# Cross attention on TensorE: the mixing products moved ahead of the next batch's key products in each slot

## The reference, cut to what matters

```python
# b = 32 batches, 100 queries, 722 context rows, 16 heads of 32
qh = (q @ wq + bq).reshape(b, -1, H, HD).transpose(0, 2, 1, 3)
kh = (k @ wk + bk).reshape(b, -1, H, HD).transpose(0, 2, 1, 3)
vh = (v @ wv + bv).reshape(b, -1, H, HD).transpose(0, 2, 1, 3)
scores = softmax(einsum('bhqd,bhkd->bhqk', qh, kh), axis=-1)
attn = einsum('bhqk,bhkd->bhqd', scores, vh)
```

## Time and profile before

| what | us |
|---|---|
| median of 3 runs | 2761.03 |
| lowest, highest | 2760.5, 2762.95 |
| the profiled execution | 2773.05 |
| its span, first to last instruction | 2771.2 |
| TensorE's matmuls busy in it | 2619.4 (95%) |
| VectorE, ScalarE busy | 1819.4 (66%), 1334.0 (48%) |

### The profile page before, as it was taken

The page is one execution under the profiler, slowest core; times in us unless marked ns, Lnnn a source line. Parts: engine busy times, 40 slices in busy tenths (PEclk is TensorE's granted clock), DMA queues, the critical chain, the costliest instruction groups (busy, mean ns, idle before and its releaser), DMA issues. The chain is left out here.

```text
span 2771.2 us, 48090 instructions
## 1 busy us (share of the span) xinstructions
PE 2619.4 (95%) x17376; PEld 2346.5 (85%) x17376; DVE 1819.4 (66%) x2867; ACT 1334.0 (48%) x2995; POOL 379.0 (14%) x276
## 2 busy tenths in 40 slices
PE   7899999999999999999999999999679999499999
PEld 7888999989999889998899988999557777388887
DVE  7477666776666776667766677666666666336665
ACT  3344555445554455554455544555333443245554
POOL 0311111111111111111111111111033333000000
PEclk9999999999999999999999999999889999659999
DMA  7654455544445444545444554454379999878983
GB/s 221 197 126 108 121 123 120 128 113 123 120 119 125 120 123 112 125 123 125 119 111 124 124 124 109 120 124 114 83 165 184 188 195 182 152 156 180 194 185 79
DMA packets 368044, 379.89 MB, mean 137 GB/s; under 512 B 128076, under 2 KB 275436, under 8 KB 367852
## 3 DMA queue, kind: packets, MB, share of 16 engines
q1 hardware_dynamic: 316732, 357.13, 55.3%
q10 hardware_dynamic: 51120, 20.11, 3.5%
HBM read 162.57 MB, written 72.57 MB: 85 GB/s over the span
## 5 line engine op out<-in xcount | busy, mean ns | idle before, releaser
L686 DVE TENSOR_TENSOR c_parted<-c_prob,c_parted 128x600 fp32r<-128x600 f32 x512 | 401.0, 783 | 429.2 <-ACT c_prob L629 429.1
L625 ACT ACTIVATE c_parted<-c_pair 128x600 fp32r<-128x600 f32 x512 | 343.9, 672 | 345.2 <-PE c_pair L763 345.1
L672 DVE TENSOR_REDUCE c_peak<-c_pair 100x1 f32<-100x724 f32 x512 | 450.4, 906 | 33.1 <-PE c_pair L745 21.7
L763 PE MATMUL c_pair<-c_q_stack,c_k_stack 100*128 100x100 f32 (+1 forms) x3072 | 381.7, 261 | 0.0
L763 PEld LDWEIGHTS c_pair<-c_q_stack,c_k_stack 100*128 100x128 f32 (+1 forms) x3072 | 369.3, 185 | 4.0
L777 PE MATMUL c_mix<-c_parted,c_v 128*66 128x200 f32 (+1 forms) x3072 | 369.7, 256 | 1.5 <-DVE c_parted L686 0.8
L607 ACT ACTIVATE c_v<-c_work 128x512 fp32r<-128x512 f32 x192 | 115.6, 602 | 481.6 <-PE c_work L91 481.6
L629 ACT ACTIVATE c_prob<-c_pair 128x600 f32<-128x600 f32 x512 | 341.0, 666 | 0.0
L777 PEld LDWEIGHTS c_mix<-c_parted,c_v 128*66 128x66 f32 (+1 forms) x3072 | 323.1, 137 | 13.9 <-DVE c_q_stack L677 0.8
L745 PE MATMUL c_pair<-c_k_stack,c_q_stack 96*100 96x362 f32 x1024 | 259.1, 334 | 3.9
L1453 ACT ACTIVATE s_prob<-s_scores,s_shift 106x100 f32<-106x100 f32 x512 | 169.7, 364 | 142.1 <-DVE s_shift L1520 142.1
(11 more groups left out here) (179 smaller groups left out, 5344.4 us busy)
## 6 DMA issues: line engine op xcount, KB each, us to landing
c_k_stack<-c_k_hi SPq DMA_DIRECT2D x1024, 90.2 KB, 2.2
e_stage<-in_ctx SPq DMA_DIRECT2D x32, 1444.0 KB, 6.4
c_k_stack<-c_k_lo SPq DMA_DIRECT2D x512, 90.2 KB, 2.1
c_q_stack<-q_parts ACTq DMA_DIRECT2D x186, 100.0 KB, 3.1
mix_parts<-c_mixed SPq DMA_DIRECT2D x64, 200.0 KB, 3.2
r_parts<-mix_parts SPq DMA_DIRECT2D x50, 256.0 KB, 4.1
s_q_stack<-qk_parts SPq DMA_DIRECT2D x16, 800.0 KB
s_k_stack<-qk_parts SPq DMA_DIRECT2D x16, 800.0 KB
```

Of the source, the lines that this page charges most:

```text
L625: act.activation(parted[i % PR][:, :, 0, :].rearrange("p (a t) s -> p a t s", a=2), logits, ACT.Exp).then_inc(exp_hi_done, 1)
L672: dve.tensor_reduce(peak[:, i:i + 1], pair[i % 2][0:S, :, 0:HALF], AX.XY, ALU.max).then_inc(peak_done, 1)
L686: dve.tensor_tensor(p[:, :, 1, :], prob[i % 2][:], p[:, :, 0, :], ALU.subtract).then_inc(p_lo_done, 1)
L763: last = pe.matmul(pair[i % 2][0:r, t // (CT // 2), col:col + S], k_stack[:, i, t * P:t * P + r], q_stack[:, i, :], start=True, stop=True)
```

## The change

In each slot the mixing piece is put directly behind the scores, and the key part behind both. All engines walk the same list, so their queues change with it.

```diff
@@ batch_plan @@
     for h in range(H + 2):
         if 0 < h < H:
             plan.append(("scores", h, 0))
+        if h >= 2:
+            plan.append(("mix", h - 2, 0))
         if with_next:
             at = sum(WORK_AFTER[:h])
             plan += KEY_WORK[at:at + WORK_AFTER[h]]
-        if h >= 2:
-            plan.append(("mix", h - 2, 0))
     return plan
```

## The result

| | before | after |
|---|---|---|
| median, 22 runs each | 2754.94 us | 2734.45 us |
| lowest of them | 2740.45 us | 2721.44 us |
| span of the profiled execution | 2771.2 us | 2733.6 us |
| cross stage in it | 1875.5 us | 1858.3 us |

The ratio is 0.9932, with a 95% interval from 0.9915 to 0.9950: between 14 and 23 us faster, 18.7 in the middle. One of the 22 runs of after took 6080.73 us and is left out of the ratio, which compares fast runs only (the median of the other 21 is 2733.87 us). The prediction said 17.9 us. A second comparison, 12 runs of after against 17 of before, gave 0.9949 (0.9922 to 0.9976). The cross stage alone gives 17.2 us in the traces.

What follows compares the result with a forecast made beforehand. TensorE's own instruction stream was taken to bound the cross stage; 12 slots x 31 batches x 0.048 us gave 17.9 us, other costs 0, so 2743.1 us from a median of 2761.03; range 2739.5 to 2751.

Steps and rivals of the forecast that it cites:

- What bounds: Cross stage: TensorE busy 34.54 of 34.54 us in the changed part, so only its own instruction stream sets the time.
- the loads' means: Changed slots: mean recorded weight loads of 185 against 137 ns, one load exchanged, gain 0.048 us per slot.
- The pair sum: Slot of three runs: three two-run periods, 1.15 + 1.57 + 1.63, less the old slot 2.20 give 2.15 us; gain 0.05.
- the runs: Slot of three runs: new order 0.68 + 0.52 + 0.94 = 2.14 us against 2.21 or 2.19; gain 0.05 to 0.07.
- The spare time of the mixing: Mixing after VectorE's difference: ready 2.83 us after the scores start, needed after 3.7 at the earliest; least spare 0.9 us.
- The key eviction before the exponential: ScalarE's queue: k_hi ends 0.92 us after the last key product starts, the exponential is due at 0.95; cost 0.
- The end of the batch: Last key run directly before the value products: k_lo ends 1.54 us after the first value load, 0.5 us remains; cost 0.
- The new wait: Exponential and difference fully behind k_hi and k_lo: 0.58 us per batch eats the gain, 1.14 gives 2778 us; chance 0.06.
- the front would take the gain back: Batch end: later k_lo delays the peak reductions and TensorE's peaks, returning at most 18.6 us, time 2762; chance 0.04.
- Half of the gain: Mixing load only partly hidden beside scores in slots with keys: 0.02 to 0.03 us per slot, 2750 to 2754; chance 0.07.
- order costs nothing inside TensorE: Slots: the 0.11 us is only moving stamps, every order costs 2.20 us and the time stays 2761; chance 0.05.
- how the numbers follow: Whole kernel: 17.9 us off the median 2761.03 gives 2743.1 us, off the profiled execution 2755.2; range 2739.5 to 2751.

Runs made afterwards that it cites:

- interleave: Kernel after with the six score and six mixing products of a slot alternating instead of in two runs; ratio to before 0.978, cross stage 1818.7 us against 1858.3.

## Why the prediction was right, and where it was wrong

- **What bounds.** Right. The phase was TensorE's own stream, and still is: the table of waits of after has the same 0.8 us for the mixing as the earlier trace rows.
- **The size.** Of the three ways to size it, the loads' means gave 0.048 us per slot. The two periods give 0.047. The pair sum (0.05) and the runs (0.05 to 0.07) had the same mechanism with more rounding. That the means came out so near was partly luck. The 185 ns of the score loads mix loads of 128 columns (192 ns) with those of the last context tile, 82 columns (153 ns), and a recorded length is not what a load costs (last section). What the change exchanges is the step of a score product: its mean over the stage is 0.113 us with a key load behind it (before) and 0.062 with a mixing load (after), a difference of 0.052. Twelve of those would be 0.62 us per batch, and the period is shorter by 0.56. The rest went in many small amounts, such as 0.1663 for 0.1658 us between two key products and 0.0931 for 0.0926 between two mixing products; what makes them is open.
- **The spare time of the mixing.** Right. The least was to be 0.9 us, for head 15. In after VectorE ends that head's low part at 596.76 + 0.79 = 597.55, and its first mixing load goes out at 598.28, as the last key product starts; the mixing product follows 0.17 later, at 598.45, so 0.90 us are to spare. For heads 5, 6, 9 and 10 the trace has 1.05 to 1.06, where the prediction has 3.9 - 2.83 = 1.07. (the earlier trace rows show head 5, not head 4 as their label says; no sum hangs on it.)

```profile
596.76 0.79 DVE L686 TENSOR_TENSOR c_parted<-c_prob,c_parted 128x600 fp32r<-128x600 f32 x1 [1.36 <-ACT c_prob L629]
...
598.28 0.67 PEld L777 LDWEIGHTS c_mix<-c_parted,c_v 128*66 128x66 f32 x6
```

- **The key eviction before the exponential.** It was to fit by 0.03 us. It does, without delay: k_hi ends as the exponential starts, 0.77 us after its scores' start (0.79 before). ScalarE's and TensorE's rows of after:

```profile
573.08 0.73 PE L763 MATMUL c_pair<-c_q_stack,c_k_stack 100*128 100x100 f32 x6
573.28 0.56 ACT L617 ACTIVATE c_k_hi<-c_work,w_key_bias 128x360 fp32r<-128x360 f32 x1 [0.35 <-PE c_work L91]
...
573.85 0.67 ACT L625 ACTIVATE c_parted<-c_pair 128x600 fp32r<-128x600 f32 x1
```

- **The end of the batch.** Predicted: k_lo ends 1.54 us after the first value load, the first peak reduction stays clear of it by 0.5 us. Measured: 600.81 + 0.59 - 599.86 = 1.54, and 0.54 us idle ahead of the peak:

```profile
600.81 0.59 DVE L666 SCALAR_TENSOR_TENSOR c_k_lo<-c_work,w_key_bias,c_k_hi 128x360 fp32r<-128x360 f32 x1 [1.04 <-ACT c_k_hi L617]
601.94 1.96 DVE L672 TENSOR_REDUCE c_peak<-c_pair 100x1 f32<-100x724 f32 x2 [0.54 <-PE c_pair L745]
```

- **Rivals.** The new wait didn't come; it came only when interleave called the mixing still earlier, behind slots 6 and 10 and in the batch without key work. That the front would take the gain back fell with the row above, and with the period: twelve slots at 0.05 gain 0.6 us and the period is shorter by 0.56, so next to nothing went back. Half of the gain would have been 0.02 to 0.03 us per slot and fell with the 0.047. That order costs nothing inside TensorE fell with the slots, and so did the rule of the Trainium skill ("TensorE: Matmul & The Clock Gate", section "The mechanism") that a load overlaps products of other row groups only. If no load ran beside a product here, a longer load would lengthen every step by the same. But 128 columns in place of 66 add 0.05 us to a step behind a product of 100 columns (0.06 to 0.11), 0.02 behind one of 200 (0.093 to 0.11) and nothing behind one of 362 (0.16 to 0.17 with either). What the prediction held against that rule, a step of 0.16 with a load recorded at 0.19, was the weaker argument, because a recorded length is no cost. The rule that a load takes columns / 1.2 ns (the Trainium skill, same page, section "LDWEIGHTS (loading the stationary operand)") agrees with the steps of 0.11 and 0.06 where loads bind (estimates from the page: 0.107 and 0.055).
- **The step that failed** is the last one, "how the numbers follow". I subtracted a gain of 17.9 us, which held, from the median of three runs, 2761.03, and gave the range 2739.5 to 2751 "a little for the runs' spread". The three runs lay within 2.5 us of each other, and I took that for the spread. The kernel before measured from 2740.45 to 2771.31 us over 22 runs with a median of 2754.94. So the base was 6 us high, and the after's median, 2734.45, fell 5 us below the range. It lies 8.7 below the forecast of 2743.1: 6.1 of that is the base, and 2.6 is that the two medians differ by 20.5 us in place of 17.9, which the interval of the ratio allows. A hint stood in front of me: the profiled execution took 12 us more than the median, and I told it only as a distance, without asking which stage could vary by that much. Of all ways to take three of those 22 runs, eight in ten have a median between 9.9 us below and 5.6 us above the median of the 22; the range should have been wider by about that much. Even that holds for one comparison only: in the two later ones the kernel before had medians of 2769.43 us (7 runs) and 2764.08 (17 runs).

## What to carry to other kernels

When TensorE has no gaps, look at the starts of its weight loads run by run: the same run that costs different amounts behind different neighbours tells what order is worth. Put behind a short product the load with the fewest columns, and behind the longest product the longest load. Pair periods, where two kinds of run alternate, give the time of an order that the trace does not contain. Judge such an edit by the length of its own stage, and give a prediction of absolute time the spread of many runs, not of three.

## What the runs showed of the hardware

A load of 128 columns took 0.11 us where it was what bound (behind products of 100 or 200 columns), one of 66 columns 0.06 behind a product of 100, and both were free behind a product of 362 columns (0.16 to 0.17 a step), all at a granted clock of 1.00. The recorded length of a load, 0.19 us for 128 columns and 0.14 for 66, is not what it costs: they went out 0.11 and 0.06 apart. The cross stage repeated within 0.4 us in 1875 while the rows stage behind it lay between 391.1 and 409.5 us in four executions with the same code there, and the self stage between 365.5 us (granted clock 0.92) and 379.6 (0.88).
